# Expert layers in blocks of 128 rows instead of 256, with the second layer two units behind the first

## What is computed

```
h = x @ down_w + down_b
probs = softmax(x @ router_w + router_b - cost); topv, topi = top_k(probs, 2); gate = softmax(topv)
for k in range(2):
    for e, (w1, b1, w2, b2) in enumerate(expert_params):
        hm = h * mask[..., e:e + 1]
        acc = acc + (gelu(gelu(hm) @ w1 + b1) @ w2 + b2)
    out = out + acc * gate[..., k:k + 1]
out = out + 0.1 * shared_expert(h)
out = out @ up_w + up_b + (gelu(x) @ core_w + core_b)
```

## Time and profile before

| | |
|---|---|
| median of 3 runs | 783.19 us (782.21 to 785.63) |
| the profiled execution | 784.58 us, span 782.7 us |
| TensorE busy | 710.9 us (91%) |
| VectorE, ScalarE, GpSimd busy | 526.8, 538.6, 499.4 us |
| granted TensorE clock, mean | 0.974 |
| expert stage | 516.1 to 736.8 us |

### The profile page before, as it was taken

How to read it: one execution, slowest core, us unless ns; L and a number is a source line. 1 busy time by engine, 2 the same in 40 slices (tenths; PEclk the granted TensorE clock), 3 DMA queues, 4 the chain that set the end, 5 groups by cost and what they waited for, 6 DMA issues and landing times.

```text
span 782.7 us, 20817 instructions
## 1 busy us (share of the span) xinstructions
PE 710.9 (91%) x6134; PEld 382.6 (49%) x6134; DVE 526.8 (67%) x834; ACT 538.6 (69%) x1113; POOL 499.4 (64%) x485
## 2 busy tenths in 40 slices
PE   1699999999999999999979989799999999999958
PEld 0122233323233332233535454368888888888624
DVE  1989999999999999988645457524444444444335
ACT  1399999999999999987526475356676677667311
POOL 5647778888888888747883454316666666566621
PEclk9999999999999999999959999799999999999979
DMA  6635666566566655343521941748788788887666
GB/s 200 214 116 184 193 193 195 193 191 201 186 205 199 185 194 180 130 165 122 165 111 52 328 154 56 242 97 120 116 133 120 116 119 122 106 101 93 114 194 234
DMA packets 137953, 124.04 MB, mean 158 GB/s; under 512 B 70164, under 2 KB 108820, under 8 KB 137880
## 3 DMA queue, kind: packets, MB, share of 16 engines
q1 hardware_dynamic: 123672, 107.50, 47.5%
q0 software_dynamic: 13632, 15.47, 13.6%
q10 hardware_dynamic: 576, 0.13, 0.1%
HBM read 60.39 MB, written 51.53 MB: 143 GB/s over the span
## 4 chain that ended last, share of the span: by engine, by line
PE 67%; DVE 8%; issue 8%; ACT 6%; DMA 5%; POOL 4%; another core or an unknown queue 1%; SPq 1%; ACTq 0%; DVEq 0%; POOLq 0%
PE EH L1175 23%; PE Y L1175 15%; PE pv L532 11%; PE ring L519 7%; PE nat L507 4%; DVE mx L653 4%; ACT P L593 3%; DMA y_sums<-ysb,to 2%; PE Y L1284 1%; DVE statx L635 1%; PE ring L551 1%; DMA rbb<-in_rb 1%; PE EH L1219 1%; PE ring L542 1%
## 5 line engine op out<-in xcount | busy, mean ns | idle before, releaser
L653 DVE TENSOR_REDUCE mx<-nat 128x2 f32<-128x1024 f32 x256 | 298.1, 1215 | 29.2 <-PE nat L507 27.6
L593 ACT ACTIVATE P<-ring 128x512 f32<-128x512 f32 x512 | 276.5, 607 | 17.7 <-PE ring L519 9.5
L1958 POOL DMA_INDIRECT y_sums<-ysb,to x84 | 138.1, 1644 | 105.7 <-DVE ysb L1878 92.9
L532 PE MATMUL pv<-P,VT 128*32 128x256 f32 x2048 | 157.6, 391 | 0.3
L519 PE MATMUL ring<-QS,KS 49*128 49x512 f16 x512 | 122.8, 391 | 15.0 <-ACT P L593 13.6
L507 PE MATMUL nat<-KS,QS 48*128 48x512 f16 x512 | 110.9, 396 | 23.5 <-DMA KS<-k_scratch 16.0
L1506 ACT ACTIVATE X<-EH,bcur 128x256 f32<-128x256 f32 x168 | 85.8, 561 | 60.1 <-PE EH L1175 27.8
L1175 PE MATMUL EH<-XA,whi 128*128 128x256 f16 x672 | 116.9, 273 | 1.2 <-DVE XB L1769 1.0
L1175 PE MATMUL Y<-whi,u 128*128 x672 | 116.9, 273 | 0.3 <-DVE u L1841 0.3
L1841 DVE TENSOR_TENSOR u<-X,u 128x512 f16<-128x512 f32 x84 | 57.8, 688 | 76.9 <-ACT u L1512 76.9
L1175 PE MATMUL EH<-XA,wlo 128*128 128x256 f16 x336 | 91.6, 273 | 0.0
(11 more groups left out here) (260 smaller groups left out, 1035.7 us busy)
## 6 DMA issues: line engine op xcount, KB each, us to landing
XA<-in_wall SPq DMA_DIRECT2D x8, 800.0 KB, 4.5
u<-in_wall SPq DMA_DIRECT2D x8, 800.0 KB, 4.5
QS<-q_scratch SPq DMA_DIRECT2D x64, 96.0 KB, 2.3
KS<-k_scratch SPq DMA_DIRECT2D x64, 96.0 KB, 2.3
X<-in_x SPq DMA_DIRECT2D x16, 256.0 KB, 2.7
X<-in_ctx_kv SPq DMA_DIRECT2D x16, 256.0 KB, 3.8
q_scratch<-qhl SPq DMA_DIRECT2D x16, 256.0 KB, 2.1
k_scratch<-khl SPq DMA_DIRECT2D x16, 256.0 KB, 3.4
```

The costliest lines, as they stand in the source:

```text
L532: m = pe.matmul(pv[32 * j:32 * j + 32, q], VT[i][:, lb, g, j, :], Pb[4 * (s % 2) + j][:, q], start=(lb == 0 and half == 0), stop=(lb == 3) ...
L593: act.activation(Pb[4 * (s % 2) + j][:, :], bank[:, :], ACT.Exp).then_inc(t_use.sem, 1)
L653: dve.tensor_reduce(mx[:, k // 8, :, k % 8], nat[k % 2][:, :, :], AX.X, ALU.max).then_inc(t_max.sem, 1)
L1958: pool.indirect_dma_start(out=ysum[:, :], out_offset=bass.IndirectOffsetOnAxis(ap=to[:, j % 2, a:a + 1], axis=0), in_=ysb[j % 2][:, a, :], ...
```

## The change

Blocks are 128 rows, units still hold up to four weight tiles, and 74 units take the place of 42. A unit's first layer is 24 matmuls of 128 columns into one bank, its second layer 12 matmuls of 256 columns. TensorE issues `output` two units behind `hidden` instead of one. ScalarE only makes four Gelus of 128 columns, and VectorE makes the high halves (`ah`) with a copy, once a unit, and one subtraction. There are four buffers of `af`, `ah` and `al`, eight of `gT` and `meta` with loads six units ahead, and one add per unit. The wait before an add is kept at two units back; the one before `to` goes from two units back to four. In the last three rounds TensorE does the rank (`rk`, `tot`) before the third core tile, and VectorE does `gl` 1 and the softmax sums after the rank. The fill rows and zeroed rows shrink to blocks of 128, and a few small tiles are shared.

```diff
-BLK = 256
+BLK = P
+AHEAD, DEEP = 6, 8
...
-            return cur(four("uT")) + core01 + cur([("lg", 0), ("h", 0), ("lt", 0), ("h", 1)]) + core2 + \
-                cur([("rk", 0)]) + (cur([("tot", 0)]) if last else []) + cur(four("rt") + [("a", 0), ("a", 1)]) + core3 + \
+            return cur(four("uT")) + core01 + cur([("lg", 0), ("h", 0), ("lt", 0), ("h", 1)]) + \
+                cur([("rk", 0)]) + (cur([("tot", 0)]) if last else []) + core2 + cur(four("rt") + [("a", 0), ("a", 1)]) + core3 + \
...
-                cur(R_(route_a)) + cur([("gl", 0), ("gl", 1)]) + cur(R_(route_p + route_b)) + (cur(R_(tables[:2])) if last else []) + \
-                cur(R_(route_c) + four("meta")) + core2 + cur([("sal", 0), ("sal", 1)]) + \
+                cur(R_(route_a)) + cur([("gl", 0)] + R_(route_b)) + (cur(R_(tables[:2])) if last else []) + \
+                cur([("gl", 1)] + R_(route_p + route_c) + four("meta")) + core2 + cur([("sal", 0), ("sal", 1)]) + \
...
+                if j >= DEEP:
+                    wait(sp, t_pe, "E", j - DEEP, "h")
+                sp.dma_start_transpose(gT[j % DEEP], gsc[bass.ds(at, BLK), 0:LAT].bitcast(F16)).then_inc(t_gt[j % DEEP].sem, 16)
+                if j >= DEEP:
+                    sp.wait_ge(t_gc.sem, t_gc.at[j - DEEP,])
+                    sp.wait_ge(t_to.sem, t_to.at[j - DEEP,])
+                sp.dma_start(meta[j % DEEP][:, :], gsc[bass.ds(at, BLK), LAT:LAT + META]).then_inc(t_mt[j % DEEP].sem, 16)
...
         def hidden(j, v):
-            wait(pe, t_gt[j % 4], j)
-            g = gT[j % 4]
-            for n in range(2):
-                if j >= 2:
-                    wait(pe, t_act, "E", j - 2, n)
-                elif n == 0:
-                    for o in ring[-4:]:
-                        read_out(*o)
-                for s in range(2):
-                    tile = 2 * n + s
-                    dst = EH[j % 2][:, n, s * BLK:(s + 1) * BLK]
-                    for k in range(2):
-                        wc = bass.ds(v + (C_W1 + tile * LAT + k * P), P)
-                        m = three(dst, wc, g[:, k, :], g[:, 2 + k, :], k == 0, k == 1)
-                m.then_inc(t_pe.sem, 1)
+            wait(pe, t_gt[j % DEEP], j)
+            g = gT[j % DEEP]
+            if j >= 4:
+                wait(pe, t_act, "E", j - 4)
+            elif j == 0:
+                for o in ring[-4:]:
+                    read_out(*o)
+            for tile in range(4):
+                dst = H[j % 4][:, tile * BLK:(tile + 1) * BLK]
+                for k in range(2):
+                    wc = bass.ds(v + (C_W1 + tile * LAT + k * P), P)
+                    m = three(dst, wc, g[:, k, :], g[:, 2 + k, :], k == 0, k == 1)
+            m.then_inc(t_pe.sem, 1)
...
+            wait(pe, t_ah, "E", j)
+            wait(pe, t_dve, "E", j)
+            for tile in range(4):
+                wc = bass.ds(v + (C_W2 + tile * LAT), LAT)
+                m = three(EY[j % 2], wc, ah[j % 4][:, tile, :], al[j % 4][:, tile, :], tile == 0, tile == 3, swap=True)
             m.then_inc(t_pe.sem, 1)
...
-            for j in range(NJ + 1):
+            for j in range(NJ + 2):
                 if j < NJ:
                     at[j] = pe.value_load(wo[0:1, j:j + 1], min_val=0, max_val=(NT - 4) * LAT)
                     hidden(j, at[j])
-                if j >= 1:
-                    output(j - 1, at[j - 1])
+                if j >= 2:
+                    output(j - 2, at[j - 2])
...
+                wait(act, t_pe, "E", j, "h")
+                if j >= 4:
+                    wait(act, t_dve, "E", j - 4)
+                    wait(act, t_ah, "E", j - 4)
+                wait(act, t_bc, j)
+                for tile in range(4):
+                    m = act.activation(af[j % 4][:, tile, :], H[j % 4][:, tile * BLK:(tile + 1) * BLK], ACT.Gelu,
+                                       bias=bcur[:, j % 2, tile:tile + 1], scale=bcur[:, j % 2, 4 + tile:5 + tile])
+                m.then_inc(t_act.sem, 1)
+                if j + 1 < NJ:
+                    columns(j + 1)
+                gates(j)
...
+            for j in range(NJ + 2):
                 if j < NJ:
...
+                    wait(dve, t_act, "E", j)
+                    if j >= 4:
+                        wait(dve, t_pe, "E", j - 4, "y")
+                    dve.tensor_copy(ah[j % 4], af[j % 4]).then_inc(t_ah.sem, 1)
+                if j >= 2:
+                    collect(j - 2)
+                if j < NJ:
+                    wait(dve, t_ah, "E", j)
+                    dve.tensor_tensor(al[j % 4], af[j % 4], ah[j % 4], ALU.subtract).then_inc(t_dve.sem, 1)
...
-            wait(dve, t_mt[j % 4], j)
-            if j >= 2:
-                wait(dve, t_ad[j % 2], j - 2)
+            wait(dve, t_mt[j % DEEP], j)
+            if j >= 4:
+                wait(dve, t_ad[j % 2], j - 4)
...
-                for a in range(2):
-                    pool.indirect_dma_start(out=ysum[:, :], out_offset=bass.IndirectOffsetOnAxis(ap=to[:, j % 2, a:a + 1], axis=0),
-                                            in_=ysb[j % 2][:, a, :], in_offset=None, compute_op=ALU.add).then_inc(t_ad[j % 2].sem, 16)
+                pool.indirect_dma_start(out=ysum[:, :], out_offset=bass.IndirectOffsetOnAxis(ap=to[:, j % 4:j % 4 + 1], axis=0),
+                                        in_=yo[j % 4], in_offset=None, compute_op=ALU.add).then_inc(t_ad[j % 2].sem, 16)
```

More of the change, by code:

```diff
@@ L850, in ffn @@
     bcur = A("bcur", [P, 2, 8])
-    meta = [A(f"meta{i}", [P, 2, META]) for i in range(4)]
-    gcur, to = A("gcur", [P, 4, 2]), A("to", [P, 2, 2], U32)
+    meta = [A(f"meta{i}", [P, META]) for i in range(DEEP)]
+    gcur, to = A("gcur", [P, 4]), A("to", [P, 4], U32)
     tmp = [v[:, :, :].rearrange("p k q -> p (k q)") for v in (uh, ul)]
@@ L891, in ffn @@
     RT = [Y[1][:, 2 * i:2 * i + 2, :].rearrange("p t q -> p (t q)").bitcast(F16) for i in range(2)]
-    EY = [Y[1][:, 2 * i:2 * i + 2, :] for i in range(2)]
+    EY = [Y[1][:, 2 * i, :] for i in range(2)]
     T = lambda n, step=1: Tally(sem(n), step)
@@ L902, in ffn @@
     t_zr = T("zero_rows", 16)
-    t_gt = [T(f"block_in{i}", 16) for i in range(4)]
-    t_mt = [T(f"meta_in{i}", 16) for i in range(4)]
+    t_gt = [T(f"block_in{i}", 16) for i in range(DEEP)]
+    t_mt = [T(f"meta_in{i}", 16) for i in range(DEEP)]
     t_ad = [T(f"y_added{i}", 16) for i in range(2)]
@@ L983, in ffn @@
     for j in range(NJ):
-        t_gt[j % 4].plan(j)
-        t_mt[j % 4].plan(j)
-        t_ad[j % 2].plan(j, n=2)
-        for n in range(2):
[L988 to L993, removed]
-    for j in range(NJ + 1):
-        if j < NJ:
-            for n in range(2):
-                t_pe.plan("E", j, "h", n)
-        if j >= 1:
-            t_pe.plan("E", j - 1, "y")
+        t_gt[j % DEEP].plan(j)
+        t_mt[j % DEEP].plan(j)
+        t_ad[j % 2].plan(j)
+        t_act.plan("E", j)
+        t_ah.plan("E", j)
+    for step in range(NJ + 2):
+        if step < NJ:
+            t_pe.plan("E", step, "h")
+        if step >= 2:
+            t_pe.plan("E", step - 2, "y")
+            t_dve.plan("E", step - 2, "y")
+        if step < NJ:
+            t_dve.plan("E", step)
     t_bc, t_gc, t_to = T("f_bcur"), T("f_gcur"), T("f_to")
@@ L1140, in rest @@
             xloads = C_ORDER[4:12]
-            for j in range(NJ - 3):
-                load(j + 3)
-                if j >= 3 and j % 3 == 0 and xloads:
+            for j in range(3, AHEAD):
+                load(j)
+            for j in range(NJ - AHEAD):
+                load(j + AHEAD)
+                if j >= 6 and j % 6 == 0 and xloads:
                     t = xloads.pop(0)
@@ L1146, in rest @@
             assert not xloads
-            wait(sp, t_pe, "E", NJ - 1, "h", 1)
+            wait(sp, t_pe, "E", NJ - 1, "h")
             for t in C_ORDER[12:]:
@@ L1320, in output @@
                     wait(pe, t_act, NG - 1, "row", t)
-            for n in range(2):
-                wait(pe, t_ah, "E", j, n)
-                wait(pe, t_dve, "E", j, n)
-                for s in range(2):
-                    tile = 2 * n + s
-                    wc = bass.ds(v + (C_W2 + tile * LAT), LAT)
-                    for a in range(2):
-                        cols = slice(a * P, a * P + P)
-                        m = three(EY[j % 2][:, a, :], wc, ah[j % 2][:, tile, cols], al[j % 2][:, tile, cols],
-                                  tile == 0 and a == 0, tile == 3, swap=True, skip=True)
+            wait(pe, t_ah, "E", j)
[3 more added lines that the diff above has]
+                m = three(EY[j % 2], wc, ah[j % 4][:, tile, :], al[j % 4][:, tile, :], tile == 0, tile == 3, swap=True)
             m.then_inc(t_pe.sem, 1)
@@ L1368, in rest @@
                     hidden(j, at[j])
-                if j >= 1:
-                    output(j - 1, at[j - 1])
+                if j >= 2:
+                    output(j - 2, at[j - 2])
             for i in (2, 3):
-                for n in range(2):
-                    wait(pe, t_act, "E", NJ - 1, n)
```

(3 more changed lines are left out.)

109 lines of the change are left out of this document (34 added, 75 removed).

## The result

The changed kernel takes **865.65 us** (median of 4 runs, 864.07 to 867.54) where the kernel before, beside it, takes 782.70 us (4 runs): ratio 1.1055, 95% interval 1.1012 to 1.1097, so 83 us slower. The profiled execution took 867.12 us.

What follows compares the result with a forecast made beforehand. TensorE's array was taken to bound the expert stage before the change, its sequencer after: 784.6 profiled + 75.3 stage + 2 tables - 3 end of stage = 858.9, less 1.4 gives 857 us; range 832 to 880.

Steps and rivals of the forecast that it cites:

- The sequencer sets the stage: Expert stage: TensorE's sequencer needs 4.0 us a unit, more than the array's 2.68, so it bounds; chance 0.82.
- Stage +75.3: Expert stage: 74 units of 4.0 us (load 0.9, twelve groups 3.08, wait 0.05) make 296 us against 220.7.
- Array 2.68 a unit and hidden: Expert stage: the array's matmuls take 1.37 us (first layer) plus 1.31 (second), hidden under the sequencer's 4.0.
- The rival of an array slower on narrow matmuls: Expert stage: 128-column matmuls take between 0.057 and 0.098 us each; about 810 us in all, chance 0.04.
- The array-pace rival: Expert stage: register operations run in the matmuls' shadow, 2.68 us a unit, stage 198 us, 760 us in all; chance 0.08.
- SyncE would be the next one late: Expert stage: at the array's pace of 2.68 us a unit, SyncE's block loads, 2.8 us apart, would come late next.
- Other engines hidden: Expert stage: ScalarE 2.4, VectorE 2.4 and GpSimd 2.05 us a unit, with SyncE's loads, stay under 4.0.
- Adds: wait met: Expert stage: an older add lands within 7.34 us, under two units' 8.0; rival of adds setting the pace, chance 0.02.
- Clock: stays at 1.00 in the stage: Expert stage: granted clock stays 1.00; rival of a fall to 1.2 GHz, 957 us, chance 0.04.
- Order in the rounds, 0 within 1: Routing rounds: rank before third core tile costs 0 us, within 1, as TensorE only exchanges two pieces of work.
- tables +2: Last routing round: five operations growing from 128x336 to 128x592 add between 0 and 2 us, taken as +2.
- End of the stage -3: After the last matmul: one add fewer and a shorter VectorE wait save 3 us, between -4.4 and 0.

Runs made afterwards that it cites:

- experiment 1: Changed kernel with fixed weight columns, so no address load and no register operation on TensorE: 772.89 us, ratio 0.9962 to the kernel before.
- experiment 3: Changed kernel with one load of four weight columns every fourth unit, without the range check: 828.81 us, ratio 1.0525 to the kernel before.
- experiment 4: Changed kernel without the third matmul of each group in the expert stage: 871.63 us, ratio 1.1065 to the kernel before.
- Experiment 2: Changed kernel with fixed weight columns, but each unit's address load and range check kept unused: 768.85 us, ratio 0.9911 to the kernel before.
- Experiment 6: Changed kernel again, unaltered: 870.01 us, ratio 1.1043; kernel before with both new orders in the rounds only: 803.26 us, ratio 1.0212.
- experiment 7: Kernel before with VectorE's new order alone: 804.39 us, ratio 1.0242; changed kernel with fixed weight columns on the same chip: 790.97 us, 1.0056.

## Why the prediction was right, and where its sizes were off

The sign, the bound and the range held: 857 was forecast, 865.65 measured. That is close partly by luck, since errors of opposite sign met: against the sum for the profiled execution (858.9, measured 867.1) the stage was 7.9 us shorter than forecast, what lies ahead of it 15.1 longer, and what follows 1.1 longer.

- **The sequencer sets the stage: right, and shown.** Experiments 1, 3 and 4 each pull at one candidate: without register operations 2.8 to 2.9 us a unit, without most of the loads 3.36, without a third of the matmuls no change.
- **Stage +75.3: measured +67.4.** The mis-sized term is the load: 0.9 us from the earlier trace rows, where the TENSOR_LOAD row itself lasted 395 ns; in the changed kernel its median is 301, and from a load to the first group pass 0.7 us (650.4 to 651.1; the median of all units is 0.76). Twelve groups and the wait between the layers took the other 3.1 to 3.2 us, where I had 3.08 + 0.05. My 0.9 was no odd pick, for in the kernel before the median over all units is as long; but single loads in it spread from 298 to 559 ns, and the earlier trace rows had two of 304 and 313:

```profile
L1367 PEldq TENSOR_LOAD <-wo x42: 298/397/559, 510.8 to 726.7; - x42
```

The step that failed is carrying the load's length over unchanged. Why it is shorter in the changed kernel no run shows.
- **Array 2.68 a unit and hidden: right.** Experiment 2 shows 1.34 + 1.31 = 2.65. The rival of an array slower on narrow matmuls is out: 0.056 each, as the earlier trace rows said for a short run.
- **The array-pace rival** (760 us if the register operations ran in the matmuls' shadow) fell as argued; its size was fair, for with fixed columns the stage was 209 to 215 us where I had 198, the rest being mostly blocks that land late (21.2 us of waits for them in experiment 1, 13.7 in experiment 2). That SyncE would be the next one late was right; its loads were not cheap enough to keep out of the way.
- **Other engines hidden: right.** In the stage's 288 us ScalarE was busy for 125, VectorE for 109 and GpSimd for 121, each waiting for the one ahead of it.
- **Adds: wait met.** Not always: GpSimd stood 55.4 us in all for older adds, with no wait of TensorE behind them.
- **Clock: stays at 1.00 in the stage: right. But the rounds were left out.** I looked for a falling clock only in the stage.
- **Order in the rounds, 0 within 1, and tables +2: measured +17.1 together.** The step that failed is "TensorE only exchanges two pieces of work". I followed TensorE's order and never VectorE's, in which the second low half moved behind the rank. Experiment 6 shows that the orders alone cost 15 us on the kernel before, experiment 7 that VectorE's alone is enough, and that on another chip both together cost less. The tables may well have been right: their five large operations take 0.77 to 0.78 us instead of 0.50 to 0.51, 1.3 us more in all, and 17.1 - 15 leaves 2; but no run asks for them alone. What joins the orders to the falling clock when both are new isn't shown, as no wait for the late low half is left then. The earlier trace rows already showed how it looks when it happens: a gap of 5.78 us at `gt` and a granted clock below 1.00.
- **End of the stage -3: measured -1.9.** The last add's landing still stands in the chain with 5.72 us:

```profile
825.37 5.72 DMA y_sums<-ysb,to
831.11 3.38 DMA acc<-y_sums
```

Open: why the clock falls in those rounds, why more on some chips than on others, and what the 4.73 us at `gt` are. A reading that fits and was only argued: the rows of the 12 matmuls of the fourth core tile begin at 424.39, and with them and the 16 behind them at twice their usual distances (12 of 0.431, 12 of 0.218 and 4 of 0.218 us) the work would end at 433.05, close to where ScalarE's copy of `gt` starts (433.32). Then the array was at 1.2 GHz some us before the clock rows say so, and the gap is slow work, not idleness.

## What to carry to other kernels

When a unit of work gets smaller, count what it keeps: here a load and 24 register operations a unit stayed while the matmuls halved, and the sequencer, hidden until then, became the bound. Its pace can be read beforehand in a place where the engine isn't held back by its array: the groups came out as read (0.257 us forecast, 0.26 measured). The load did not: 397 ns in the kernel before and 301 in the changed one, medians over many units, so such a term needs bounds from several places, not one number. And an order changed "in passing" on one engine has to be followed to what the next engine waits for, on its own: 15 of some 82 us were lost by it here.

## What the runs showed of the hardware

- A register operation on TensorE's sequencer is recorded with 46 or 32 ns, but takes 0.13 us on the mean from start to start (24 from 651.1 to 654.1). Where a third of the matmuls between them was gone it was no less (twelve groups in 2.86 us from first to last in both, experiment 4).
- The load of a value into a register in each of 74 units cost nothing while the sequencer was ahead of the array (experiment 2). Where it was behind, one load for four units, without the range check, saved 42 us in 74 units, 0.57 each (experiment 3).
- One load of four values lasted 333 ns; the median of loads of one value was 301 ns in the changed kernel, and 308 to 397 in the kernel before and in the runs of experiments 2 and 4.
- The same program on different chips: 772.9 and 791.0 us for the kernel with fixed columns, with stretches at 1.2 GHz in rounds 1 and 2 on the slower one and in neither of them on the other. In rounds 0 and 3 both had one.
